# Attention's output projection from split operands, a smaller tiling of the inverse, and other places for some loads

## What is computed

```python
x = x + delta_rule(layernorm(x))   # 8 heads of 128, causal conv, 2 Householder steps a token, gate, Wo
x = x + ffn(layernorm(x))          # 256 -> 512 -> 512 -> 256, relu
x = x + attention(layernorm(x))    # 16 query heads in 4 groups, head size 128
x = x + ffn(layernorm(x))          # the same weights again
```

```python
gate, delta = (x @ Wq) @ Wg, (x @ Wv) @ Wd
bias = (sigmoid(gate) * delta).transpose(0, 2, 1)
logits = scores * scale + bias            # masked: causal, and bias > 0
o = softmax(logits) @ v
return o.reshape(b, s, 16 * 128) @ Wo     # the output projection
```

## Time and profile before

| | us |
|---|---|
| median of three runs | 4434.16 (4428.42 to 4441.27) |
| the profiled execution, whole | 4430.39 |
| its span | 4428.5 |
| TensorE busy | 4126.1 (93%) |
| VectorE busy | 2977.5 (67%) |
| ScalarE busy | 2185.5 (49%) |
| GpSimd busy | 1582.6 (36%) |
| DMA | 321.37 MB, 73 GB/s over the span |

### The profile page before, as it was taken

How to read it: one execution, slowest core, us unless ns; L and a number is a source line. 1 busy time by engine, 2 the same in 40 slices (tenths; PEclk the granted TensorE clock), 3 DMA queues, 4 the chain that set the end, 5 groups by cost and what they waited for, 6 DMA issues and landing times. The chain is left out here.

```text
span 4428.5 us, 96953 instructions
## 1 busy us (share of the span) xinstructions
PE 4126.1 (93%) x32143; PEld 3443.9 (78%) x32143; DVE 2977.5 (67%) x7897; ACT 2185.5 (49%) x5661; POOL 1582.6 (36%) x2836
## 2 busy tenths in 40 slices
PE   4699999999999999999999689789999999999979
PEld 3488888888888888888888578767777777777768
DVE  4577777777777777777777354346776776776655
ACT  2355555555555555555555144334444444444444
POOL 0466666666666666666666100000000000000000
PEclk9999999999999999999999699979999999999989
DMA  3333333333333333333333232121111111111021
GB/s 134 92 80 89 79 80 89 87 91 88 79 90 83 79 89 79 89 84 91 92 79 83 71 120 86 58 63 47 52 32 53 52 47 37 52 47 47 10 69 34
DMA packets 545328, 321.37 MB, mean 73 GB/s; under 512 B 251584, under 2 KB 503488, under 8 KB 543296
## 3 DMA queue, kind: packets, MB, share of 16 engines
q1 hardware_dynamic: 544832, 315.12, 25.0%
HBM read 230.95 MB, written 83.98 MB: 71 GB/s over the span
## 5 line engine op out<-in xcount | busy, mean ns | idle before, releaser
L938 DVE SCALAR_TENSOR_TENSOR g_conv<-g_r,g_taps,g_conv 128x511 f32<-128x511 f32 (+2 forms) x961 | 699.0, 741 | 133.9 <-ACT g_conv L821 125.4
L825 ACT ACTIVATE g_us<-g_chn 128x128 f32<-128x128 f32 x528 | 146.6, 278 | 678.2 <-PE g_chn L620 677.4
L1990 ACT ACTIVATE a_pr<-a_pr,a_low 128x128 f32<-128x128 f32 (+3 forms) x512 | 286.5, 560 | 391.1 <-DVE a_low L2135 375.0
L2295 POOL TENSOR_TENSOR a_dg<-a_const,a_fl 128x384 fp32r<-128x384 f32 x32 | 26.5, 827 | 1156.2 <-DVE a_fl L2142 1156.2
L545 PE MATMUL g_r<-g_x_hi,g_w_hi 128*128 128x512 f32 x770 | 365.8, 475 | 9.7 <-issue 7.4
L2135 DVE CUSTOM_DVE_ANT_0 a_pr<-a_sc,a_bias 128x128 f32<-128x128 f32 (+3 forms) x512 | 242.0, 485 | 191.0 <-issue 172.2
L545 PE MATMUL g_r<-g_x_hi,g_w_lo 128*128 128x512 f32 x770 | 306.2, 398 | 0.0
L545 PE MATMUL g_r<-g_x_lo,g_w_hi 128*128 128x512 f32 x770 | 304.0, 395 | 0.0
L1809 PE MATMUL a_out<-a_pt,a_v 128*128 128x512 f32 (+3 forms) x1024 | 298.0, 434 | 0.9 <-DVE a_oT L2155 0.9
L1138 POOL TENSOR_TENSOR g_prod<-g_small 64x14 f32<-64x14 f32 (+6 forms) x896 | 227.7, 254 | 170.1 <-DMA g_small<-lower_d 104.4
L821 ACT ACTIVATE g_conv<-g_r,g_taps 128x512 f32<-128x512 f32 x321 | 220.5, 687 | 135.9 <-PE g_r L545 124.8
(11 more groups left out here) (357 smaller groups left out, 12085.3 us busy)
## 6 DMA issues: line engine op xcount, KB each, us to landing
g_w_raw<-w_heads SPq DMA_DIRECT2D x66, 768.0 KB, 4.9
lower_d<-g_L SPq DMA_DIRECT2D x64, 512.0 KB, 3.4
g_T<-low_d SPq DMA_DIRECT2D x64, 512.0 KB, 5.1
g_U<-upp_d SPq DMA_DIRECT2D x64, 512.0 KB, 6.4
a_w<-w_groups SPq DMA_DIRECT2D x32, 640.0 KB, 4.6
oT_d<-g_oT SPq DMA_DIRECT2D x67, 256.0 KB, 6.4
f_oT<-oT_d SPq DMA_DIRECT2D x8, 2048.0 KB, 8.5
a_wo<-wo_b SPq DMA_DIRECT2D x32, 512.0 KB, 5.4
```

The lines of the kernel that those rows point to most:

```text
L938: ins = V.scalar_tensor_tensor(out=y[:, k:L], in0=x[:, 0:L - k], scalar=tap, in1=y[:, k:L], op0=ALU.mult, op1=ALU.add)
L1990: A(pr[g % 2][:, i, 0:width(i)], pr[g % 2][:, i, 0:width(i)], ACT.Exp, scale=-1.0, bias=low[g % 2][:, i:i + 1], accum_out=tot[g % 2][:, i: ...
```

## The change

Four parts.

1. *Attention's projection.* `oT` (now two buffers of 128x512, by the parity of the head) and `wo` (now one buffer) are split into `o_hi`, `o_lo`, `wo_hi`, `wo_lo`, which are single buffered. `project_out` makes 48 fp32r matmuls a turn. ScalarE gets `head_high` and `wo_high`, VectorE `head_low` and `wo_low`.
2. *Weights of gate and delta.* The two weight products are made in `build_tables` and handed on in DRAM (`gd_d`). Attention loads them, and only the constants that it uses.
3. *The inverse.* Level 4 uses four tiles of 32x32 on the diagonal (`BLOCKS`) with 16 columns in place of two of 64x64 with 32; the masks are laid out for it.
4. *Feed-forward.* With `delta_out`, x is loaded after the weights and heads of the output projection. Without, the layernorm stands ahead of the split of the first weights on ScalarE and VectorE.

Its core (the declarations of new buffers and semaphores are left out):

```diff
@@ build_tables, SP @@
+            for to, name in ((wq, "wqT"), (wv, "wvT"), (wg, "wg"), (wd, "wd")):
+                sp.dma_start(to[:], io[name].rearrange("(p n) d -> p n d", p=P)).then_inc(s["t_gw"], 16)
             for par in (0, 1):
                 turn(B - 2 + par, par, False)
             store_rows(B, 1)
+            sp.wait_ge(s["t_gd"], 1)
+            sp.dma_start(io["gd_d"], gd[:].rearrange("p k n -> p (k n)")).then_inc(s["t_out0"], 16)
             sp.wait_ge(s["t_glo"], 1)
@@ build_tables, PE @@
+            pe.wait_ge(s["t_gw"], 64)
+            for k in range(KD):
+                for first, w, v, many in ((0, wq, wg, NQ), (HKV, wv, wd, HKV)):
...
+                        mm = nc.tensor.matmul(ps_ab[:, at:at + HKV], w[:, n, k * P:(k + 1) * P], v[:, n, :], start=(n == 0), stop=(n == many - 1))
+            mm.then_inc(s["t_gm"], 1)
             pe.wait_ge(s["t_g"], 1)
@@ delta_rule @@
+        BLOCKS = {l: [slice(i, i + (2 << l)) for i in range(0, P, 2 << l)] for l in LEVELS[:-1]}
@@ lev_nu, PE @@
-                    for r in QUADS:
-                        mm = M.matmul(lev[hf][r, c, 0:HCOL].rearrange("p (j n) -> p j n", n=1 << l), Lm[o][r, hf * HC + c, r],
-                                      seconds(U[o][r, hf * HC + c, r], l), start=True, stop=True)
+                    for r in BLOCKS[l]:
+                        mm = M.matmul(lev[hf][r, c, 0:1 << l], Lm[o][r, hf * HC + c, r], U[o][r, hf * HC + c, r.start + (1 << l):r.stop], start=True, stop=True)
@@ lev_add, DVE @@
-                    for r in QUADS:
-                        to = blk(half(U[o], hf)[r, :, r], l, 1)
-                        ins = V.tensor_tensor(to, to, packed(lev[hf][r, :, 0:HCOL], l), ALU.add)
+                    for r in BLOCKS[l]:
+                        to = half(U[o], hf)[r, :, r.start + (1 << l):r.stop]
+                        ins = V.tensor_tensor(to, to, lev[hf][r, :, 0:1 << l], ALU.add)
@@ feed_forward, SP @@
-            load(0, 0)
-            if delta_out:
+            if not delta_out:
+                load(0, 0)
+            else:
                 sp.dma_start(raw_a[:, 0:H * D].rearrange("p (h d) -> p h d", h=H), rows_of("wo_a")).then_inc(s["wo_in"], 16)
                 load_heads(0)
+                load(0, 0)
@@ feed_forward, ACT (and the same on DVE) @@
-            split(0)
             if delta_out:
+                split(0)
...
-            norm(0)
+                norm(0)
+            else:
+                norm(0)
+                split(0)
@@ attention, SP @@
-                if not (isinstance(t, int) and t < 2):
-                    sp.wait_ge(s["y"], 2 * t - 2)
-                load_wo(n, n % 2)
+                if not begin:
+                    sp.wait_ge(s["wo_lo"], t)
+                load_wo(n)
@@ attention, PE @@
             def project_out(t, tp_, half):
                 if half == 0:
-                    pe.wait_ge(s["oT"], G * t + G)
+                    pe.wait_ge(s["o_lo"], G * t + G)
+                    pe.wait_ge(s["wo_lo"], t + 1)
                 for j, m in enumerate((2 * half, 2 * half + 1)):
-                    for g in range(G):
-                        mm = M.matmul(pb[:, j * D:(j + 1) * D], oT[tp_][:, g, m * P:(m + 1) * P], wo[tp_][:, g, :], start=(g == 0), stop=(g == G - 1))
+                    at = slice(m * P, (m + 1) * P)
+                    mm = product(pb[:, j * D:(j + 1) * D], [(o_hi[:, g, at], o_lo[:, g, at], wo_hi[:, g, :], wo_lo[:, g, :]) for g in range(G)])
                 mm.then_inc(s["y"], 1)
-            pe.wait_ge(s["in"], 16 * 6)
...
-            mm.then_inc(s["gd"], 1)
+            pe.wait_ge(s["in"], 32)
@@ attention, ACT @@
+            def head_high(t, g):
+                act.wait_ge(s["oT"], G * t + g + 1)
+                A(o_hi[:, g, :], oT[g % 2][:], ACT.Copy).then_inc(s["o_hi"], 1)
+
+            def wo_high(t):
+                act.wait_ge(s["wo"], 16 * t + 16)
+                A(wo_hi[:], wo[:], ACT.Copy).then_inc(s["wo_hi"], 1)
...
                 evac(t, 0)
+                if not begin:
+                    head_high(t - 1, G - 1)
...
                     split_w(t + 2, here)
+                if not begin:
+                    act.wait_ge(s["y"], 2 * t)
+                head_high(t, 0)
+                head_high(t, 1)
...
                 evac(t, 3)
+                wo_high(t)
+                head_high(t, 2)
@@ attention, DVE @@
+                if not (isinstance(t, int) and G * t + g < 2):
+                    dve.wait_ge(s["o_lo"], G * t + g - 1)
+                V.tensor_tensor(oT[g % 2][:], out[:], tl[tp_][:], ALU.add).then_inc(s["oT"], 1)
+
+            def head_low(t, g):
+                dve.wait_ge(s["o_hi"], G * t + g + 1)
+                V.tensor_tensor(o_lo[:, g, :], oT[g % 2][:], o_hi[:, g, :], ALU.subtract).then_inc(s["o_lo"], 1)
+
+            def wo_low(t):
+                dve.wait_ge(s["wo_hi"], t + 1)
+                V.tensor_tensor(wo_lo[:], wo[:], wo_hi[:], ALU.subtract).then_inc(s["wo_lo"], 1)
...
                 normalise(t, 2)
+                if not begin:
+                    head_low(t - 1, G - 1)
                 head_out(t, here, 0)
...
                     query(t + 1, 1)
+                head_low(t, 0)
                 evac(t, 3)
                 if nxt:
                     normalise(t + 1, 0)
+                head_low(t, 1)
                 head_out(t, here, 2)
+                wo_low(t)
+                head_low(t, 2)
```

More of the change, by code:

```diff
@@ L70, in constants @@
         s = 1 << l
[L71 to L74, removed]
+        for at in range(0, P, 2 * s):
+            lev[at:at + s, i, 0:s] = -1.0
     put("levels", lev.reshape(P, len(LEVELS) * C))
@@ L226, in _ @@
                     mm.then_inc(s["t_ab"], 1)
+            pe.wait_ge(s["t_sig"], B + 1)
+            pe.wait_ge(s["t_gw"], 64)
+            for k in range(KD):
+                for first, w, v, many in ((0, wq, wg, NQ), (HKV, wv, wd, HKV)):
+                    at = k * 2 * HKV + first
+                    for n in range(many):
+                        mm = nc.tensor.matmul(ps_ab[:, at:at + HKV], w[:, n, k * P:(k + 1) * P], v[:, n, :], start=(n == 0), stop=(n == many - 1))
+            mm.then_inc(s["t_gm"], 1)
             pe.wait_ge(s["t_g"], 1)
@@ L583, in lev_un @@
                         continue
-                    for r in QUADS:
-                        mm = M.matmul(lev[hf][r, c, 0:HCOL], T[r, hf * HC + c, r], nu[r, hf * HC + c, 0:HCOL], start=True, stop=True)
+                    l = LEVELS[li]
+                    for r in BLOCKS[l]:
+                        mm = M.matmul(lev[hf][r, c, 0:1 << l], T[r, hf * HC + c, r], nu[r, hf * HC + c, 0:1 << l], start=True, stop=True)
                 mm.then_inc(s["d_un"], 1)
@@ L1533, in _ @@
             dve.wait_ge(s["eps"], 1)
-            split(0)
             if delta_out:
+                split(0)
                 heads(0, range(H))
                 split(1)
-            norm(0, 0)
+                norm(0, 0)
+            else:
+                norm(0, 0)
+                split(0)
             columns(0)
@@ L1590, in attention @@
         s = {n: sems[f"a_{n}"] for n in ATTN_SEMS}
-        const = sb("const", [P, NCONST])
-        cc = {k: const[:, lo:hi] for k, (lo, hi) in CONSTS.items()}
+        USED = CONSTS["pick_group"][1]
+        const = sb("const", [P, USED])
+        cc = {k: const[:, lo:hi] for k, (lo, hi) in CONSTS.items() if hi <= USED}
         ident = cc["ident"]
@@ L1604, in attention @@
         wv_hi, wv_lo = (sb(f"wv_{i}", [P, KD, NK * P], F32R) for i in ("hi", "lo"))
-        wo = two("wo", [P, G, D])
+        wo = sb("wo", [P, G, D])
+        wo_hi, wo_lo = (sb(f"wo_{i}", [P, G, D], F32R) for i in ("hi", "lo"))
         xl, x, xn = sb("xl", [P, TT, D]), two("x", [P, TT, D]), sb("xn", [P, TT, D])
@@ L1621, in attention @@
         pt = two("pt", [P, L * TT - P * 6])
-        oT = two("oT", [P, G, L])
+        oT = two("oT", [P, L])
+        o_hi, o_lo = (sb(f"o_{i}", [P, G, L], F32R) for i in ("hi", "lo"))
         sc = [ps(f"sc{i}", [P, L]) for i in (0, 1)]
@@ L1877, in turn @@
                 if not begin:
-                    pe.wait_ge(s[f"wo{there}"], wo_count(t, n))
                     if n == 0 or not more:
@@ L1917, in _ @@
             pe.wait_ge(s["one"], 1)
-            pe.wait_ge(s["in"], 16 * 6)
-            wqT = [t[:].rearrange("p m (j d) -> p (m j) d", d=D) for t in pr]
-            wvT = bias[1][:, 0:2, :].rearrange("p m (j d) -> p (m j) d", d=D)
-            for k in range(KD):
-                at = slice(k * P, (k + 1) * P)
-                for n in range(NQ):
-                    mm = M.matmul(tp[0][:, k * HKV:(k + 1) * HKV], wqT[n * 2 // NQ][:, n % (NQ // 2), at], wg[:, n, :], start=(n == 0), stop=(n == NQ - 1))
-                for n in range(NK):
-                    mm = M.matmul(tp[1][:, k * HKV:(k + 1) * HKV], wvT[:, n, at], wd[:, n, :], start=(n == 0), stop=(n == NK - 1))
-            mm.then_inc(s["gd"], 1)
+            pe.wait_ge(s["in"], 32)
```

(2 more changed lines are left out.)

59 lines of the change are left out of this document (24 added, 35 removed).

## The result

The changed kernel takes 4561.55 us (median of four runs, 4558.89 to 4566.64), the kernel before, run beside it, 4433.99 us. The ratio is 1.0281 (95% interval 1.0266 to 1.0296): 2.8% or 127.6 us slower. Forecast were 4513 us, 1.8% slower, in a range of 4445 to 4620. The profiled execution has a span of 4560.3 us, 131.8 us more than before.

A forecast was written before the change was run, and what follows sets the result against it. VectorE was taken to bound attention's dense stretch ahead of head 1's logits, though idle a third of the stage. Terms: -37 + 83 + 49 + 30 - 24.5 + 0 - 17 - 5 = +78.5 us, giving 4513 us; range 4445 to 4620.

The forecast's parts named there:

- Item 1: Attention's projection: 48 fp32r matmuls replace 16 fp32 products a turn, each half 0.58 us shorter, -37 us.
- item 3: Attention's projection: its first half now waits for VectorE's last head split, behind normalise(t,2), +49 us (bounds 35 and 60).
- Item 2: Attention: VectorE's splits ahead of head 1's logits delay TensorE's third score tile, +83 us (bounds +60 and +90).
- Item 4: Attention: gaps of about 3 us lower TensorE's clock in 20 turns, +30 us (bounds 0 and 53).
- Items 5 and 6: Attention's start: transposes earlier without the weight products, -24.5 us; tables stage hides those products in a wait, 0 us.
- Item 7: Delta rule, first inverse level: bursts on 32x32 tiles 0.21 us shorter, partly offset by more additions, -17 us.
- rival B: Delta rule's small tiles: records start no sooner than 29 ns apart, +120 in place of -17, 4650 us; chance 0.15.
- Item 8: First and last feed-forward: reordered loads and earlier normalisation, together -5 us (bounds -8 and 0).
- A: Attention: splits fit VectorE's idle time, so the added waits and clock loss cost nothing, 4350 us; chance 0.09.
- C: Whole kernel: the attention costs and inverse level all come out low, no change to measure, 4433 us; chance 0.06.

The follow-up runs named there:

- experiment 7: Changed kernel with VectorE's five splits moved between score tiles' logits, four oT buffers instead of two, some ScalarE copies moved later: 4358.07 us, ratio 0.9833 to the kernel before.
- 1: Changed kernel with attention's projection put back to that of the kernel before, other three parts kept: 4401.77 us, ratio 0.9917 to the kernel before.
- experiment 3: Changed kernel with the last head's VectorE split moved from behind normalise(t,2) to between head 2's second and third logits: 4508.73 us, ratio 1.0157 to the kernel before.
- experiment 5: Changed kernel with TensorE making head 1's query product three times instead of once in every turn: 4524.6 us, ratio 1.0192 to the kernel before.
- experiment 9: Kernel before with only the 32x32 tiles at level 4 of the inverse: 4432.55 us, ratio 0.9995.
- experiment 2: Kernel before with only the split projection added: 4590.28 us, ratio 1.0345.

## Why the forecast was right, point by point

The direction, the stage and the two waits were right, the sum 49 us too low. By its own steps:

| step | forecast, us | measured, us | how |
|---|---|---|---|
| 1, shorter products | -37 | -44 | experiment 7 against 1, 31 turns |
| 2, splits ahead of head 1 | +83 | +96 | idle time ahead of its third tile, 5.2 to 101.7 |
| 3, wait ahead of the projection | +49 | +44 to 53 | idle time; experiment 3 |
| 4, clock | +30 | 40 to 53 | what is left of the 31 turns: 146 - 137 + 44; experiment 5 |
| 5, attention's start | -24.5 | -23 | start to first flags, 68.1 to 44.8 |
| 7, levels | -17 | +3, none | stage; experiment 9 |
| 8, order of loads | -5 | 0 | both stages |

*Item 1* was right in its mechanism, and only its size was off. The new stream starts most of its matmuls 0.113 us apart, not 0.120 as in the feed-forward. The last two rows here are such a pair; the first three are item 3's place, where VectorE goes from `normalise` to `o_lo` to the first matmul, as forecast:

```profile
3509.05 1.27 DVE L2197 TENSOR_SCALAR a_pr<-a_pr,a_rec 128x128 f32<-128x128 f32 x4
3510.24 0.69 DVE L2183 TENSOR_TENSOR a_o_lo<-a_oT,a_o_hi 128x512 fp32r<-128x512 f32 x1
...
3511.03 0.35 PE L1753 MATMUL a_pb<-a_wo_hi,a_o_hi 128*128 128x256 f32 x1 [1.18 <-issue]
...
3479.08 0.28 PE L1753 MATMUL a_pb<-a_wo_hi,a_o_hi 128*128 128x256 f32 x1
3479.19 0.28 PE L1753 MATMUL a_pb<-a_wo_hi,a_o_lo 128*128 128x256 f32 x1
```

TensorE stood for 1.18 us here. The forecast was 1.30 in 23 turns and 2.51 in 8. I find 1.2 in 24 and 2.4 in 7. The trace of the kernel before has the same 24 and 7 (offsets of 0.56 and 1.77 us); the forecast's sum of 25.8 us is that of the trace, only its two counts are off by one.

*Item 2* sized the added stretch at 3.03 us; it is 3.25 (7.64 less 4.39). The excess is in the first `o_lo`: 0.92 us at 3486.99, where the others of its size take 0.68. In the forecast's account the slack of 11.3 us was taken off in whole. The 2.0 us in every fourth turn are that slack. In two turns the wait was 4.9 us; there VectorE stood idle itself, at most 2.5 us, released by nothing that the profile shows.

*Item 4* was the right mechanism, too small. I had taken one stretch at half clock for 1.7 us and 20 of them. The time at half clock in the turns rose by 100 us, which is some 30 stretches of 3.4 us; work done at half speed takes double, so each costs up to 1.7 us: 50 us. By experiment 5, where 73 us less of it gave 28 us, it would be nearer 40. Experiment 5 shows that the gap ahead of head 1 brings the clock down: with it filled, half of that time goes. The shorter waits ahead of the projection did not, as far as experiment 3 shows: without them that time did not fall.

*Items 5 and 6* held. The transposes start 12.5 us into the stage, and the tables stage hides the products, with a wait of 7 us left (forecast: about 6). First attention's start, then the tables stage:

```profile
2877.86 1.38 DVE L2101 TENSOR_SCALAR a_xn<-a_xl,a_mv,a_rstd 128x256 f32<-128x256 f32 x4
...
2879.39 1.09 PE L1760 MATMUL a_pa<-a_const,a_xn 128*128 128x128 f32 x4 [19.23 <-DVE a_xn L2101]
...
117.60 2.07 PE L245 MATMUL t_ps_tab<-t_g,t_const 64*128 64x512 f32 x2 [7.02 <-DVE t_g L330]
```

*Item 7* failed in one term. The matmuls themselves came as forecast: 32 of them go out in 0.26 us (forecast 0.23) and rival B is out. But the next instruction starts 0.51 us after the burst's start, where it was 0.585 with 16 large ones: the burst drains for 0.25 us in place of 0.15. The gain is 0.07 us a burst, not 0.21. The additions cost 216 ns each (forecast 224; eight of them are 1.8 us and four of the old ones 1.1, where the forecast has 1.9 and 1.2), and TensorE's next transposes now wait 0.4 us for them in every turn, 25.6 us in all. The rows are the burst, the instruction behind it, the same instruction behind a burst of the kernel before (which starts at 1004.43 in the earlier trace rows), the additions by shape and that wait:

```profile
1005.98 0.44 PE L576 MATMUL g_lev<-g_U,g_L 32*32 32x16 f32 x32
1006.49 0.38 PE L632 MATMUL g_chn<-g_R,g_U 128*128 128x128 f32 x1
...
1005.01 0.38 PE L620 MATMUL g_chn<-g_R,g_U 128*128 128x128 f32 x1
...
L976 DVE TENSOR_TENSOR g_U<-g_U,g_lev 32x64 f32<-32x64 f32 x520 | 112.2, 216 | 7.2
...
PEld g_lev L604 <- DVE g_U L976: 25.6, 64, 0.4
```

On the Trainium skill's rule ("TensorEngine Tiling (Array Packing)", Performance Considerations: about 60 cycles of overhead for each matmul): the measured distance of 8 ns from start to start in this burst is a third of what 60 cycles would be at 2.4 GHz (25 ns, an estimate from the page's figure), so the trace does not agree with it for matmuls on different tiles. A single tile gets a matmul only every fourth start, 34 ns apart, which the rule would allow. What the Trainium skill says in the same page's Key Properties, that different tiles work in parallel, agrees with the trace.

*Item 8* gave nothing that the two stages show; no run has this part alone. In the last feed-forward the normalisation does start early, but the scaling of x now falls beside GpSimd's addition and takes 3.69 us where it took 1.76. Together with ScalarE's table load, which now stands between the statistics and the scaling, this gives most of the gain back: the first layer starts 15.7 us into the stage, before 16.2, and the stage is 0.9 us longer. The last row is the scaling in the kernel before.

```profile
4351.29 1.81 DVE L1491 BATCH_NORM_STATS2 h_stats<-h_x 128x6 f32<-128x256 f32 x4
...
4355.28 2.34 POOL L1578 TENSOR_TENSOR h_xb<-h_x,h_b 128x1024 f32<-128x1024 f32 x1 [8.04 <-DMA h_b<-b]
4355.44 3.69 DVE L1499 TENSOR_SCALAR h_xn<-h_x,h_mv,h_rstd 128x256 f32<-128x256 f32 x4
...
4362.84 0.76 PE L1322 MATMUL h_hid<-h_xT_hi,h_w_hi 128*128 128x512 f32 x1 [1.50 <-DVE h_xT_lo L1506]
...
4227.05 1.76 DVE L1481 TENSOR_SCALAR h_xn<-h_x,h_mv,h_rstd 128x256 f32<-128x256 f32 x4
```

*The rivals.* A (the splits hide) is what experiment 7 made true, by moving them; in the changed kernel's order it was false, as the stretch without a hole said. B is refuted by the burst's row. C needed items 2, 3, 4 and 7 all low; none was (96, 44 to 53, 40 to 53 and about 0 us).

One thing in the text ahead of the prediction was put loosely: the inverse's last level joins two blocks of 64, so the matrices are of 128 rows (64 tokens by two steps), not of 64.

## What to carry to other kernels

Before an engine gets more work, ask where in its order that stands. An engine that is idle for a third of a stage can have no slack at one place, and idle time at another is no help unless the work is put there: with the same five subtractions a turn, the split projection cost 160 us (154 by experiment 2) when they stood ahead of the next head's logits, and gained 44 us when they stood in the waits between score tiles (both against the kernel without it). A buffer that is reused sooner than needed also fixes that order; two more buffers of 256 KB, with the order that they allow, were worth 58 us here. And a wait of 3 us on TensorE costs more than 3 us, if its clock falls behind it.

## What the runs showed of the hardware that was not expected

- Matmuls on four 32x32 tiles start 8 ns apart (32 in 0.26 us), but the instruction behind them waits until 0.51 us after the first; with 16 on two 64x64 tiles it was 0.585 us.
- Some VectorE instructions took longer while GpSimd ran: `h_xn` 3.69 us for four instead of 1.76, `o_lo` 0.92 instead of 0.68 us. Others did not: in the kernel before, three `h_stats` beside the same addition of GpSimd took 1.35 us, in the changed one four without it 1.81. That GpSimd is the cause was not tested by a run of its own.
- Work put into TensorE's idle time made the kernel faster: 86 us more of it, 37 us less time.
